# A masked attention kernel: five row buffers, constants on ScalarE's queue, and every mask added by TensorE in quarters

## What is computed

```python
h = jnp.maximum(_layernorm(x, axis=-1), 0.0)                 # x is 4096 x 256
neib_att = jnp.tanh(neigh @ Wn1 + bn1) @ Wn2 + bn2           # 4096 x 32
value    = neigh @ Wv + bv                                   # 4096 x 128
x_att    = jnp.tanh(h @ Wx1 + bx1) @ Wx2 + bx2               # 4096 x 32
ws = jax.nn.leaky_relu(jnp.einsum('nh,mh->nm', x_att, neib_att), negative_slope=0.01)
ws = jnp.where(adj > 0, ws, jnp.float32(-9e15))              # adj is 4096 x 4096, int32
ws = jax.nn.softmax(ws, axis=1)
out = x + jnp.concatenate([h @ Wfx + bfx, ws @ value], axis=1)
```

## Time and profile before

| | us |
|---|---|
| median of 3 runs | 514.41 |
| the three runs | 516.66, 514.41, 512.79 |
| the profiled execution, its own time | 515.66 |
| its span, which all rows below divide | 513.9 |
| mean granted clock of PE in it | 0.987 of full speed |

### The profile page before, as it was taken

The page is one execution under the profiler, slowest core; times in us unless marked ns, Lnnn a source line. Parts: engine busy times, 40 slices in busy tenths (PEclk is TensorE's granted clock), DMA queues, the critical chain, the costliest instruction groups (busy, mean ns, idle before and its releaser), DMA issues.

```text
span 513.9 us, 8883 instructions
## 1 busy us (share of the span) xinstructions
PE 479.7 (93%) x2813; PEld 368.3 (72%) x2855; DVE 432.8 (84%) x843; ACT 436.2 (85%) x625; POOL 214.0 (42%) x340
## 2 busy tenths in 40 slices
PE   5797889799999999999999999999999999998996
PEld 4354667577878777877787778777777787766884
DVE  1559979789989998999998999899998989984654
ACT  2645699999989998999999989998999989996552
POOL 1602113235654456455654564456444544440100
PEclk8879999999999999999999999999999999999999
DMA  6854885565545844575566636655575456500100
GB/s 179 197 159 115 147 156 89 115 116 93 83 81 102 168 75 73 121 164 83 83 119 133 106 61 122 139 104 84 103 144 84 79 81 138 90 5 0 42 1 22
DMA packets 38530, 52.07 MB, mean 101 GB/s; under 512 B 4436, under 2 KB 30292, under 8 KB 38484
## 3 DMA queue, kind: packets, MB, share of 16 engines
q0 software_dynamic: 9216, 33.56, 40.3%
q1 hardware_dynamic: 29268, 17.95, 11.8%
HBM read 80.86 MB, written 4.19 MB: 166 GB/s over the span
## 4 chain that ended last, share of the span: by engine, by line
PE 68%; issue 6%; ACT 4%; DVE 2%; POOL 1%; DVEq 0%; ACTq 0%; POOLq 0%
PE ps_turned L916 20%; PE ps_scores L893 10%; PE ps_product L935 10%; PE ps_product L937 10%; PE ps_product L936 10%; PE ps_scores L892 3%; ACT pt_hi L504 2%; PE ps_product L861 2%; DVE pt_lo L674 1%; ACT scores L528 1%; PE ps_product L839 1%; PE ps_product L853 1%; POOL scores L416 1%; PE ps_product L846 1%; PE ps_product L946 1%
## 5 line engine op out<-in xcount | busy, mean ns | idle before, releaser
L674 DVE TENSOR_TENSOR pt_lo<-ps_turned,pt_hi 128x512 fp32r<-128x512 f32 x256 | 172.3, 685 | 36.7 <-ACT pt_hi L504 20.8
L416 POOL TENSOR_TENSOR scores<-scores,mask 128x512 f32<-128x512 f32 x109 | 127.8, 1173 | 170.6 <-ACT scores L528 170.4
L504 ACT ACTIVATE pt_hi<-ps_turned 128x512 fp32r<-128x512 f32 x256 | 157.1, 615 | 33.7 <-PE ps_turned L916 32.6
L916 PE MATMUL ps_turned<-ident,scores 128*128 128x128 f32 x1024 | 156.3, 275 | 2.9 <-DVE pt_lo L674 2.5
L916 PEld LDWEIGHTS ps_turned<-ident,scores 128*128 128x128 f32 x1024 | 121.7, 140 | 48.4 <-DVE pt_lo L674 25.7
L528 ACT ACTIVATE scores<-ps_scores 128x1024 f32<-128x1024 f32 x128 | 133.2, 1040 | 8.9 <-PE ps_scores L893 8.7
L893 PE MATMUL ps_scores<-neib,xs 128*128 128x512 f32 x256 | 135.5, 538 | 2.7 <-DVE mask L661 2.3
L540 ACT ACTIVATE scores<-scores,neg_top 128x2048 f32<-128x2048 f32 x64 | 129.4, 2022 | 0.0
L692 DVE CUSTOM_DVE_ANT_0 scores<-ps_scores,scores,top 128x1024 f32<-128x1024 f32 x96 | 122.6, 1277 | 3.1 <-issue 1.4
L935 PE MATMUL ps_product<-pt_hi,v_hi 128*128 128x512 f32 x256 | 113.2, 442 | 0.2 <-DVE pt_lo L674 0.2
L937 PE MATMUL ps_product<-pt_lo,v_hi 128*128 128x512 f32 x256 | 101.2, 396 | 0.0
(11 more groups left out here) (77 smaller groups left out, 380.6 us busy)
## 6 DMA issues: line engine op xcount, KB each, us to landing
adj_in<-in_adj POOLq DMA_DIRECT2D x64, 512.0 KB, 5.5
scores<-in_L_gnn_neigh SPq DMA_DIRECT2D x8, 512.0 KB, 5.5
x_rows<-in_x SPq DMA_DIRECT2D x8, 512.0 KB, 5.5
x_left<-in_x SPq DMA_DIRECT2D x8, 256.0 KB, 2.9
x_right<-in_x SPq DMA_DIRECT2D x8, 256.0 KB, 4.4
out_h<-x_left SPq DMA_DIRECT2D x8, 256.0 KB, 2.7
out_h<-x_right SPq DMA_DIRECT2D x8, 256.0 KB, 4.5
scores<-in_x SPq DMA_DIRECT2D x1, 512.0 KB, 3.9
```

The costliest lines, as they stand in the source:

```text
L416: pool.tensor_tensor(half, half, mask[:, s % MASK_RING, BANK:CHUNK], ALU.add).then_inc(masked, 1)
L504: act.activation(pt_hi[:, (2 * b + u) % HI_RING], pt[:, u], ACT.Copy).then_inc(hi_done, 1)
L674: dve.tensor_tensor(pt_lo[:, u], pt[:, u], pt_hi[:, (2 * b + u) % HI_RING].bitcast(FP32), ALU.subtract).then_inc(lo_done, 1)
L916: last = pe.transpose(pt[:, u, i * P:(i + 1) * P], scores[:, parity * TILES + i, n * P:(n + 1) * P], ident[:, :])
```

## The change

It has six parts.

1. `neigh` rows get five buffers (`ROWS_RING`), so that SP queues five groups before the first has been turned, and a load waits for the turn five groups before. `w1_n`, `w1_x`, `b1` and `b2` are loaded on ACT's queue.
2. The hidden layer of `neigh` is laid out as that of x already was: the first layer writes four tiles of 32 partitions, tanh covers 128 columns, the second layer is four fp32 matmuls with block-diagonal weights. The rounded copy and the remainder of the hidden layer go, `att_high` moves from DVE to ACT.
3. `adj` chunks 4 to 7 get buffers of their own in a score buffer not yet used (`adj_front`), and the first four `adj` loads are issued by GpSimd when rows 4, 5, 6 and 7 of `neigh` have landed (`PACE`).
4. `POOL_MASKS` becomes `STEPS`, so GpSimd adds no mask. PE adds each mask as four matmuls of 256 columns, one behind each transpose of `turn(s, 0)`; where no transposes are due, the four stand alone. The waits for `mask_done` and `leaked` move with the first quarter.
5. PE, ACT and DVE get another order inside a step.
6. The steps at which the next group of x is loaded, normalised, turned and so on are moved.

```diff
-X_LOAD = -10
-X_STATS = (-6, -6, -5, -4)
-X_AGGR = -4
+X_LOAD = -7
+X_STATS = (-6, -6, -4, -4)
+X_AGGR = -3
-X_NORM = (0, 2, 4, 4)
-X_TURN = (6, 7)
-X_FIRST, X_TANH = 9, 11
+X_NORM = (2, 2, 4, 4)
+X_TURN = (6, 8)
+X_FIRST, X_TANH = 11, 11
...
-X_LEFT_LOAD, X_SUM = 4, (8, 18)
-X_RIGHT = 8
+X_LEFT_LOAD, X_SUM = 11, (18, 19)
+X_RIGHT = 4
-POOL_MASKS = BACK_LAG
+POOL_MASKS = STEPS
+MASK_PART = CHUNK // TILES
+MASK_TURN = 0
...
             load_neigh(0)
...
             load_neigh(1)
             load_x_rows(0)
...
+            load_neigh(2)
+            sp.wait_ge(cleared, 2)
+            load_w2(0, w2_n, wn2)
+            load_neigh(3)
+            load_neigh(4)
+            load_w2(1, w2_x, wx2)
             sp.dma_start(x_ahead, x_tiles[:, TILES:2 * TILES, :]).then_inc(x_ahead_in, 16)
...
-            for e in range(2, NEIGH_GROUPS):
-                sp.wait_ge(turned, KT * (e - 1))
+            for e in range(ROWS_RING, NEIGH_GROUPS):
+                sp.wait_ge(turned, KT * (e - ROWS_RING + 1))
                 load_neigh(e)
...
+            for n, e in zip(range(0, ADJ_RING + FRONT, LOAD), PACE):
+                pool.wait_ge(rows_in[e % ROWS_RING], 16 * (e // ROWS_RING + 1))
+                load_adj(n)
...
+            def att_high(par, q):
+                if q == 0:
+                    act.wait_ge(b2_in, B2_IN)
+                act.wait_ge(second_done, q + 1)
+                act.activation(neib[:, q * GROUP:(q + 1) * GROUP], ps_att[par], ACT.Identity,
+                               bias=b2[:, 0:1]).then_inc(att_hi, 1)
...
                 act.wait_ge(first_done, q + 1)
-                wait(act, hidden_lo, q - 1)
+                wait(act, second_done, q - 1)
                 act.activation(hidden[:, par], ps_hidden, ACT.Tanh, bias=b1[:, 0:1]).then_inc(hidden_done, 1)
-                act.wait_ge(hidden_done, q + 1)
-                wait(act, second_done, q - 1)
-                act.activation(hidden_stack[:, par], hidden[:, par], ACT.Copy).then_inc(hidden_hi, 1)
...
             def step(s):
+                hi(s, 0)
                 aggregate(s)
-                hi(s, 0)
                 rise(s)
...
             def step(s):
-                if s < POOL_MASKS:
+                if s < BACK_LAG:
                     mask_of(s + 2)
                 leak(s)
                 lo(s, 0)
+                x_work(s)
+                neigh_rest(s)
+                negate(s)
+                if BACK_LAG <= s < STEPS - 2:
+                    mask_of(s + 2)
                 close(s)
-                negate(s)
-                x_work(s)
                 lo(s, 1)
-                if POOL_MASKS <= s < STEPS - 2:
-                    mask_of(s + 2)
-                neigh_rest(s)
...
+            def first_layer(q):
...
+                for k in range(KT):
+                    for i in range(TILES):
+                        last = pe.matmul(ps_hidden[i * D_HID:(i + 1) * D_HID, :], w1_n[:, k, :],
+                                         rows_t[:, q, k * GROUP + i * P:k * GROUP + (i + 1) * P],
+                                         start=k == 0, stop=k == KT - 1)
...
-                pe.matmul(ps_att[par], w2_stack, hidden_stack[:, par], start=True, stop=True).then_inc(second_done, 1)
+                for i in range(TILES):
+                    last = pe.matmul(ps_att[par][:, i * P:(i + 1) * P], w2_n[:, i, :], hidden[:, par],
+                                     start=True, stop=True)
+                last.then_inc(second_done, 1)
...
+            def mask_add(s, i):
...
+                if i == 0:
+                    pe.wait_ge(mask_done, s + 1)
+                    if s >= 2:
+                        pe.wait_ge(leaked, s - 1)
...
+                part = slice(i * MASK_PART, (i + 1) * MASK_PART)
+                pe.matmul(ps[:, s % 2, part], ident_bf16, mask[:, s % MASK_RING, part],
+                          start=i % 2 == 0, stop=False)
...
-                on_pool = h == 1 and s >= POOL_MASKS
-                if not on_pool:
-                    pe.matmul(ps[:, s % 2, half], ident_bf16, mask[:, s % MASK_RING, half], start=True, stop=False)
                 last = pe.matmul(ps[:, s % 2, half], xs[:, parity, tile * P:(tile + 1) * P],
-                                 neib[:, c * CHUNK + h * BANK:c * CHUNK + (h + 1) * BANK], start=on_pool, stop=True)
+                                 neib[:, c * CHUNK + h * BANK:c * CHUNK + (h + 1) * BANK],
+                                 start=h == 1 and s >= POOL_MASKS, stop=True)
...
                 for i in range(TILES):
                     last = pe.transpose(pt[:, u, i * P:(i + 1) * P],
                                         scores[:, parity * TILES + i, n * P:(n + 1) * P], ident[:, :])
+                    if u == MASK_TURN:
+                        mask_add(s, i)
                 last.then_inc(block_turned, 1)
...
             def step(s):
+                turn(s, 0)
                 score(s, 0)
-                turn(s, 0)
                 score(s, 1)
                 product(s, -2)
                 turn(s, 1)
+                side(s)
                 product(s, -1)
                 agg_turn(s)
-                side(s)
```

More of the change, by code:

```diff
@@ L143, in scratch @@
             return ap.rearrange(f"p ({names}) -> p {names}", **sizes)
[L145 to L153, removed]
+        rows = [scratch(4, i * TILES * D_IN, TILES, D_IN) for i in range(4)] + [scratch(5, 0, TILES, D_IN)]
+        x_ahead = scratch(5, 1024, TILES, D_IN)
+        hidden = scratch(5, 2048, 2, P)
+        w1_n = scratch(5, 2304, KT, D_HID)
+        w2_n = scratch(5, 2560, TILES, P)
+        w_v = scratch(5, 3072, KT, D_OUT)
+        adj_front = scores[:, 3, 0:FRONT * CHUNK // 2].bitcast(BF16).rearrange("p (a n) -> p a n", n=CHUNK)
         rows_t = scores[:, 6:8, :].rearrange("p a (g n) -> p (a g) n", n=KT * GROUP)
@@ L191, in build @@
         adj_ready = [sem(f"adj_ready{i}") for i in range(ADJ_RING // LOAD)]
+        front_ready = [sem(f"front_ready{i}") for i in range(FRONT // LOAD)]
         mask_done = sem("mask_done")
@@ L249, in load_neigh, with load_w2 @@
             def load_neigh(e):
-                par = e % 2
-                sp.dma_start(rows[:, par], neigh_tiles[:, bass.ds(e * TILES, TILES), :]).then_inc(rows_in[par], 16)
+                slot = e % ROWS_RING
+                sp.dma_start(rows[slot], neigh_tiles[:, e * TILES:(e + 1) * TILES, :]).then_inc(rows_in[slot], 16)
+            def load_w2(side, w, w_in):
+                for j in range(TILES):
+                    sp.dma_start(w[j * D_HID:(j + 1) * D_HID, j, :].rearrange("p (r h) -> p r h", h=D_HID),
+                                 w_in.rearrange("p (a h) -> p a h", a=1).to_broadcast(
+                                     [D_HID, P // D_HID, D_HID])).then_inc(w2_in[side], 16)
             def load_x_rows(e):
@@ L611, in neigh_step @@
                         mask_of(n)
-                first = e == 0
-                if not first:
-                    att_high(1 - par, q - 1)
-                dve.wait_ge(hidden_hi, q + 1)
-                low = hidden_stack[P // 2:P, par]
-                dve.tensor_tensor(low, hidden[P // 2:P, par], low.bitcast(FP32), ALU.subtract).then_inc(hidden_lo, 1)
-                if not first:
+                if e > 0:
                     att_low(1 - par, q - 1)
@@ L795, in neigh_step @@
                     turn_rows(q + 1, e + 1)
-                pe.wait_ge(turned_out, KT * (q + 1))
-                wait(pe, hidden_done, q)
-                for k in range(KT):
-                    last = pe.matmul(ps_hidden, w1_n[:, k, :],
-                                     rows_t[:, bass.ds(q, 1), k * GROUP:(k + 1) * GROUP].rearrange("p a n -> p (a n)"),
-                                     start=k == 0, stop=k == KT - 1)
-                last.then_inc(first_done, 1)
-                if e == 1:
-                    pe.wait_ge(w2_done, 1)
+                first_layer(q)
                 if e > 0:
                     second_layer(1 - par, q - 1)
-                if e == 1:
-                    pe.wait_ge(consts_in[1], CONSTS_IN[1])
+                if e == TURN_X:
+                    pe.wait_ge(w1_in[1], 16)
+                    pe.wait_ge(w2_in[1], W2_IN)
                     for k in range(KT):
```

146 lines of the change are left out of this document (69 added, 77 removed).

## The result

| | us |
|---|---|
| before, median of 14 runs | 514.62 (512.00 to 517.51) |
| after, median of 14 runs | 519.26 (518.36 to 520.28) |
| ratio, 95% interval | 1.0102, 1.0086 to 1.0119 |
| span of the profiled execution, before and after | 513.9, 518.5 |

The changed kernel is 1.0% slower. The forecast was 510, 0.9% faster: the time lies in the range, on the wrong side of no change.

What follows compares the result with a forecast made beforehand. PE was taken to pace the loop, with ACT and DVE little behind. Front -11.9, steps 0 to 18 -2.5 and loop +9.6 sum to -4.8 us; from the 514.41 median that gives 509.6, said as 510, range 496 to 522.

Steps and rivals of the forecast that it cites:

- The quarters: PE's loop: each 256-column mask matmul between transposes costs 0.108 us, bounded by 0.05 and 0.21.
- (a): Rival, PE's loop: quarters slip in between transposes at 0.05 us each, period near 52.8, total 491; 10%.
- (d): Rival, PE's loop: changes between fp32 transpose and bf16 mask leave weight loads open, 0.21 a quarter, about 565; 8%.
- The price of the masks on PE: Loop: four quarters for one 512-column mask add 0.20 us a step, 3.2 a group; PE's floor becomes 54.8.
- What the period does: Loop: 0.8 of 2.6 us of loss a group stays, period 55.6, +1.4 a group, +9.6 us in all.
- (c): Rival, loop: a quarter's wait for `leaked` or ACT's uneven steps keep the loss at 2.6, +21.6, total 522; 15%.
- Costed at nothing: the swaps inside ACT's and DVE's steps: Loop: reordering these steps costs 0; a DVE step of 3.15 us would have to grow past 3.4 to count.
- The wait for `shift`: Loop: ACT's waits for GpSimd, 6.4 us in five, go, since GpSimd has no adds between its small instructions.
- The front: Before the first score: last `neigh` row lands at 30.1, first score at 35.4 instead of 47.28, -11.9 us.
- Six issues, while ACT waits for its first turn: Front: the constants' loads go down ACT's queue while ACT waits for its first turn.
- Steps 0 to 18: Between first score and loop: bias adds and a split leave DVE, 2.3 us; -2.5 us in all (0 to -4).
- The tail: After the last rise: transposes and products alone, 55.9 us, unchanged.

Runs made afterwards that it cites:

- e8: Changed kernel with every mask quarter from step 19 on issued twice on PE: 562.31 us, 1.0931 of the kernel before.
- e5: Kernel before with every mask on PE as 512-column matmuls ahead of their scores, all orders and the front as before: 524.69 us, ratio 1.0194.
- e15: Changed kernel with PE's old step order and masks as 512 columns ahead of their scores: 514.79 us, 1.0023 of the kernel before.
- e2: Changed kernel with masks as two 512-column matmuls ahead of their scores, none between transposes: 519.82 us, 1.0121 of the kernel before.
- e14: e13 with PE's step alone in the changed order: 523.93 us, 1.0193 of the kernel before.
- e13: e6 with PE adding both halves of every mask as 512 columns, GpSimd none: 514.29 us, 1.0014 of the kernel before.
- e9: Changed kernel with DVE's step alone back in its old order: 522.21 us, 1.0154 of the kernel before.
- e10: Changed kernel with the old steps for x (loading, normalising, turning and so on): 521.66 us, 1.0153 of the kernel before.
- e11: e6, with PE adding both mask halves in the last two steps of each group of 16: 500.41 us, 0.9729 of the kernel before.
- e4: Changed kernel with a semaphore for each first-layer bias, so ACT's second copy waits only for that of neigh: 518.17 us, 1.0092 of the kernel before.
- e16: e11 with GpSimd's first sum on x_right put off to step 2: 501.03 us, 0.9754 of the kernel before.
- e3: Changed kernel with no mask added from step 19 on, so its output is not the reference's: 494.64 us, 0.9638 of the kernel before.
- e12: e6 with DVE's step alone in the changed order: 522.39 us, 1.0155 of the kernel before.
- e6: Changed front with two bias semaphores, and the loop of the kernel before (half of the masks on GpSimd): 504.19 us, 0.9798 of the kernel before.

## Why the prediction was wrong, point by point

**The quarters: right.** Forecast 0.108 each, measured 0.109 from start to start and 0.098 as an addition (e8). Rivals (a) and (d) fall with it: no pair of transpose and quarter stood near 0.16, and of 258 between 150 and 450 us 20 were above 0.24 (the longest 0.276), too few for (d). With (a) falls the transpose mode's factor of four for FP32 (the Trainium skill, TensorE: Matmul & The Clock Gate, Terms): if it holds here, it left no room for a quarter.

**The price of the masks on PE: right.** The forecast was +9.6 for the loop from PE's count and 0.8 us of loss left in a period. e5, which is the move without the rest, gave +10.3 and a period of 55.54 where I had 55.6. (The loop is 108 steps, or 6.75 groups, and not 6.67; with that the term is 9.7.)

**"What the period does": the step that failed.** I kept 0.8 of the 2.6 us of loss for the whole of the change, and for PE's new order I had only a check on `leaked`: beyond that it stood at nothing. That check was sound (PE waited for it 4.4 us in the whole execution). The turn's other wait, for `lo`, I did not look at, though the earlier trace rows had it as the largest idle time ahead of a turn. PE's order costs 5.2 us (e15 against e2), 10.3 with the old orders of DVE and ACT and the old steps of x (e14 against e13). Rival (c) had the place, idle PE ahead of a turn, but by `leaked` and with 2.6 us of loss; by the forecast's own floor of 54.8 the loss was 1.1 a group.

**"Costed at nothing: the swaps inside ACT's and DVE's steps": wrong as well, in the change's favour.** DVE's order is worth 2.8 us and the new steps of x 2.6 (e9, e10), under PE's new order; under the old one both together, with ACT's, are worth 0.5 (e15 against e13). My test for DVE's order was one of throughput: a step of DVE may grow to 3.4 us. The order changed no length here; it changed when `lo` is ready. The loop's +14.4 is 10.3 for the masks and 4.1 for what the orders leave together. ACT's order by itself was not tried.

**The wait for `shift`: right, and small.** It is gone after. e11 buys the same for two masks in sixteen.

**The front: the second step that failed. It was right in direction, 3.1 us too much, and paced by something else.** The last row was forecast to land at 30.1. It landed at 22.56, and was turned only at 31.58; from there to the first score I had 5.3 and it took 38.85 - 31.58 = 7.3. By the first score the gain is 47.28 - 38.85 = 8.4, which is 3.5 short. PE's turns after:

```profile
17.78 1.23 PE L781 MATMUL ps_turned<-ident,scores 128*128 128x128 f32 x8
20.51 1.04 PE L781 MATMUL ps_turned<-ident,scores 128*128 128x128 f32 x8
23.05 1.04 PE L781 MATMUL ps_turned<-ident,scores 128*128 128x128 f32 x8
26.52 1.06 PE L781 MATMUL ps_turned<-ident,scores 128*128 128x128 f32 x8 [0.78 <-ACT scores L451]
...
31.58 1.09 PE L781 MATMUL ps_turned<-ident,scores 128*128 128x128 f32 x8
```

None of these waits for a row. The queues moved 277 GB/s in 10 to 20 us, the last three rows landed 1.4 to 1.5 us apart and ahead of all `adj` loads, where I had 1.77 us each and three of those loads in front of the last, and PE with ACT became the pace: 2.5 to 2.7 us a row, then 3.5 and 5.1 where the first group of x is worked in between. I had priced PE at 2.3 a row and left that group's work out. Waits in the front hid one behind another: the bias (4.50 us, e4 gave 0.8, since the third row landed only at 11.93), the masks beside GpSimd's sum (e16 took 0.5 off the masks and gave 0.1), and a chain of x that I did not break. So the excess of 2.0 behind the last turn stays open in its parts. "Six issues, while ACT waits for its first turn" was wrong as well: ACT issued until 6.2, loaded its table at 6.24 and copied the first turn at 7.53, where the kernel before did so at 5.57:

```profile
0.72 1.28 ACT L439 ACT_TABLE_LOAD   x1 [0.72 <-PEq L992]
5.57 1.09 ACT L439 ACTIVATE scores<-ps_turned 128x512 f32<-128x512 f32 x2 [3.56 <-PE ps_turned L780]
```

**Steps 0 to 18: half.** -1.3 against -2.5. The 10 us from 50 are not the same steps in both kernels: they begin 1.6 us behind the first rise before and 10.4 behind it after. The stretch after that matches the earlier trace rows's is this one:

```profile
41.20:51.20 10.00, 8.84 (x71) 7.98 (x70) 9.82 (x20) 5.92 (x9) 0.53 (x1) 1.00 0.68 129
```

DVE is the bound there as before, with 9.82 of 10 us; what it lost in work let ACT do more in the same time (5.92 us for 4.04), and from 50 on ACT is full with 10.00. The same code gave -3.1 and -0.4 in e3 and e8, so the size isn't firm.

**The tail: right**, +0.3 us.

The forecast's sum had +9.6 for the loop and -14.4 ahead of it; it was +14.4 and -10.1. Either miss alone would have left a time within 1% of before; the two together made it 4.6 us slower.

## What to carry to other kernels

When the order inside a step changes, list for each engine the waits of the instruction that is moved forward and how long the awaited buffer had been ready; a busy share of 99% hides a wait that sits at the edge. An order can be fitted to a placement: DVE's new order earned 2.8 us in the changed kernel, where GpSimd adds no masks, and cost 18.7 with GpSimd adding, so try parts in both settings. Take the large move in small doses too: two masks of sixteen on the bound engine bought a wait and 4 us, all sixteen cost ten.

## What the runs showed of the hardware

- A bf16 matmul of 256 columns between fp32 transposes costs 0.098 to 0.109 us, and the change of operand type at every instruction leaves no weight load open.
- A DVE mask of 0.42 us stretches to as much as 1.4 beside a GpSimd add of 1.17 and ends 0.28 us behind it (49 of 51 in e12); masks of over 0.8 us are 6 of 103 or 38 of 98, by DVE's order alone (e6, e12).
- DMAs issued by ACT delay its first table load: 0.72 before, 6.24 us after, for six issues of 0.5 to 2 us.
